# A gated cross-attention stage ahead of six transformer layers: two pairs of groups in a loop become four groups in one written order

## The reference

```python
x = x + tanh(g_xattn[0]) * xattn(layernorm(x), ctx_1024, Wq, bq, qk_b, Wv, bv)
x = x + tanh(g_ffn[0]) * six_layers(layernorm(x), ...)

def xattn(query, value, Wq, bq, qk_b, Wv, bv):
    q = einsum('bsd,ed->bse', query, Wq) + bq + qk_b
    v = einsum('bsd,ed->bse', value, Wv) + bv
    scores = einsum('bqd,bkd->bqk', q, v) / sqrt(128 / 16)
    attn = softmax(scores, axis=-1)
    return einsum('bqk,bkd->bqd', attn, v)
```

## Time and profile before

| what | us or share |
|---|---|
| median of 3 runs (lowest, highest) | 1567.43 (1566.67, 1567.67) |
| the profiled execution's own time | 1565.26 |
| its span, first to last instruction | 1563.4 |
| busy in the span: PE, DVE, ACT, POOL | 96%, 84%, 75%, 76% |
| mean granted clock of PE | 0.983 of 2.4 GHz |

### The profile page before, as it was taken

One profiled execution on the slowest core, in us unless ns is written; L12 is line 12 of the kernel. 1 busy time (PEld: TensorE's weight loads), 2 busy tenths in 40 slices (PEclk: granted clock), 3 DMA queues, 4 the chain that ended last, 5 costly groups with the idle time before them and its releaser, 6 DMA issues.

```text
span 1563.4 us, 80230 instructions
## 1 busy us (share of the span) xinstructions
PE 1499.3 (96%) x31136; PEld 1251.6 (80%) x31136; DVE 1317.1 (84%) x2497; ACT 1167.1 (75%) x2333; POOL 1180.8 (76%) x1166
## 2 busy tenths in 40 slices
PE   4489999999999999999999999999999999999997
PEld 3367888888888888888888888888888888888886
DVE  3578889888888988988888898888889889889883
ACT  3457788788778778877877887887787787777774
POOL 1277877878887887788788878888878877877781
PEclk8789999999999999999999999999999999999998
DMA  5111111011111111101012110112111012010101
GB/s 147 43 43 32 29 37 43 26 50 55 36 30 32 43 40 59 42 27 36 26 43 62 36 42 26 36 32 72 30 32 30 20 31 64 23 30 20 30 25 34
DMA packets 41462, 62.40 MB, mean 40 GB/s; under 512 B 3662, under 2 KB 30412, under 8 KB 41420
## 3 DMA queue, kind: packets, MB, share of 16 engines
q1 hardware_dynamic: 41420, 61.84, 13.5%
HBM read 18.84 MB, written 1.05 MB: 13 GB/s over the span
## 4 chain that ended last, share of the span: by engine, by line
PE 92%; issue 1%; ACT 1%; DVE 0%; POOL 0%; ACTq 0%; DVEq 0%; POOLq 0%
PE bank L1035 16%; PE bank L1105 12%; PE bank L1117 11%; PE bank L1028 10%; PE bank L1029 9%; PE bank L1030 8%; PE bank L1078 8%; PE bank L1152 5%; PE bank L1141 3%; PE bank L1060 3%; PE bank L1142 2%; PE bank L1143 2%; PE bank L1131 1%; PE bank L1125 1%; PE bank L1014 0%
## 5 line engine op out<-in xcount | busy, mean ns | idle before, releaser
L406 POOL TENSOR_TENSOR u<-u,t 128x512 f32<-128x512 f32 x384 | 490.4, 1282 | 23.8 <-DVE t L821 23.8
L420 POOL TENSOR_TENSOR u<-u,rn 128x512 f32<-128x512 f32 x384 | 392.7, 1044 | 75.8 <-ACT rn L572 75.8
L426 POOL TENSOR_TENSOR P<-P,rs 128x512 f32<-128x512 f32 x192 | 196.3, 1043 | 123.6 <-DVE rs L845 123.6
L821 DVE TENSOR_TENSOR t<-bank,TS 128x512 f32<-128x512 f32 x384 | 258.3, 683 | 28.4 <-ACT sq L561 25.8
L1028 PE MATMUL bank<-Wl,xsh 128*128 (+1 forms) x576 | 273.6, 475 | 5.8 <-POOL xsl L400 3.0
L812 DVE TENSOR_TENSOR u<-bank,TC 128x512 f32<-128x512 f32 x384 | 262.1, 683 | 10.1 <-issue 6.5
L805 DVE TENSOR_REDUCE ss<-sq 128x8 f32<-128x512 f32 x384 | 250.5, 673 | 2.9 <-ACT sq L561 2.9
L1029 PE MATMUL bank<-Wh,xsl 128*128 (+1 forms) x576 | 228.4, 397 | 0.0
L1030 PE MATMUL bank<-Wh,xsh 128*128 (+1 forms) x576 | 227.9, 396 | 0.0
L561 ACT ACTIVATE sq<-bank 128x512 f32<-128x512 f32 x384 | 221.5, 605 | 6.2 <-PE bank L1030 5.7
L1035 PE MATMUL bank<-shape_constants,u 128*128 128x128 f32 x1536 | 219.0, 275 | 3.3 <-POOL u L420 3.2
(11 more groups left out here) (102 smaller groups left out, 2960.4 us busy)
## 6 DMA issues: line engine op xcount, KB each, us to landing
vs<-v SPq DMA_DIRECT2D x96, 384.0 KB, 3.3
Wraw<-in_L_ffn_Wqkv_dram SPq DMA_DIRECT2D x72, 117.5 KB, 2.1
WoS<-in_L_ffn_Wo_dram SPq DMA_DIRECT2D x6, 512.0 KB, 3.7
W1h<-Wh SPq DMA_DIRECT2D x6, 341.0 KB, 2.5
W1l<-Wl SPq DMA_DIRECT2D x6, 341.0 KB, 2.9
Wraw<-in_L_ffn_W_dram SPq DMA_DIRECT2D x12, 116.0 KB, 2.2
OT<-in_x_dram SPq DMA_DIRECT2D x2, 512.0 KB, 5.7
v<-in_ctx_dram SPq DMA_DIRECT2D x2, 512.0 KB, 7.0
```

The costliest lines, as they stand in the source:

```text
L406: nc.gpsimd.tensor_tensor(u[:, r, c], u[:, r, c], t2[:, r, c % 2], ALU.add).then_inc(add_done[c], 1)
L420: nc.gpsimd.tensor_tensor(by_head(u[:, r, c]), by_head(u[:, r, c]), spread(rn[:, r, HC * c:HC * c + HC], HC, DH), ALU.mult).then_inc(qk_re ...
L821: nc.vector.tensor_tensor(halves(t2[:, r, c % 2]), halves(bank_of("chunk", c, r)[:])[:, :, ::-1, :], TS[:, layer(it - lag), c % 2].broadca ...
```

## The change

The loop goes. Four groups g = 0 to 3 of four items have temporary tiles and two banks each: `CROSS_A` takes turned x, queries, scores, turned probabilities and the last turn; `CROSS_B` the turned values, the straight values and the attention. Each engine has one written list of steps over all four groups, and every wait counts groups. The arithmetic of a group is the same, instruction by instruction.

- **Inputs in parts.** SP issues eleven transfers ahead of the raw blocks where it were seven: x and context as groups 0, 1, and 2 with 3; the gates, the values' bias and the scales of `ev` apart. PE waits for `fc` and `sc`, DVE for `fc`, ACT for the gates and then `sc`.
- **Context read in place.** PE reads `ctxS`; POOL's copies to `cT` go.
- **POOL** clears `vs[0:32]` (DVE did) and makes the rotary tables at the start, then the eight lower parts, one after another.
- **ACT** takes the upper parts 0 to 3 behind the second group's turned probabilities and 4 to 7 among the last steps, each behind its own block.

The core of the diff (lines that only rename waits and some of the new helpers, which hold the old instructions, are left out):

```diff
-        cT = [t2[:, 0, g] for g in range(2)]
-        slots = [[u[:, g, j] for j in range(NCH)] + [PT[:, 0, g], kT[:, g].rearrange("p t n -> p (t n)")] + [sq[:, g]]
-                 for g in range(2)]
-        xh4, xhT4, qT4, vT4, p4, pT4, v4 = ([slots[g][j] for g in range(2)] for j in range(7))
-        st4 = sb("st4", [128, 2, GB, 6])
-        mv4 = sb("mv4", [128, 2, GB, 2])
-        lv4 = sb("lv4", [128, 2, GB])
-        rstd4 = sb("rstd4", [128, 2, GB])
-        mx4 = sb("mx4", [128, 2, GB])
-        nm4 = sb("nm4", [128, 2, GB])
-        sum4 = sb("sum4", [128, 2, GB])
-        rc4 = sb("rc4", [128, 2, GB])
-        rg4 = sb("rg4", [128, 2, GB])
+        xh4, xhT4 = ([u[:, k, g] for g in range(GROUPS)] for k in range(2))
+        qT4 = [t2[:, g // 2, g % 2] for g in range(GROUPS)]
+        vT4 = [(qT, kT)[g % 2][:, g // 2].rearrange("p t n -> p (t n)") for g in range(GROUPS)]
+        v4 = [PT[:, g // 2, g % 2] for g in range(GROUPS)]
+        p4, pT4 = xh4, xhT4
...
+        CROSS_A, CROSS_B = K[0:4], K[4:8]
...
+        def rows(t, g):
+            return [t[:, GB * g + k] for k in range(GB)]
...
+        def arrived(eng, sems_of_parts, g):
+            eng.wait_ge(sems_of_parts[min(g, 2)], 16)
...
+            def items(t, dst, how, a, b, done):
+                sp.dma_start(dst[:, a:b], t[a:b].rearrange(how)).then_inc(done, 16)
+
+            items(x, H, "b s d -> s b d", 0, GB, x_in[0])
+            sp.dma_start(ev[:, 128:130], every_token[128:130].partition_broadcast(128)).then_inc(gate_in, 16)
+            sp.dma_start(fc[:], by_feature).then_inc(features_in, 16)
+            items(ctxT, ctxS, "b d s -> d b s", 0, GB, ctx_in[0])
+            sp.dma_start(sc[:], shape_consts).then_inc(shapes_in, 16)
+            items(x, H, "b s d -> s b d", GB, 2 * GB, x_in[1])
+            items(ctxT, ctxS, "b d s -> d b s", GB, 2 * GB, ctx_in[1])
+            sp.dma_start(ev[:, 0:128], every_token[0:128].partition_broadcast(128)).then_inc(rows_in, 16)
+            sp.dma_start(ev[:, 130:], every_token[130:].partition_broadcast(128)).then_inc(rows_in, 16)
+            items(x, H, "b s d -> s b d", 2 * GB, NB, x_in[2])
+            items(ctxT, ctxS, "b d s -> d b s", 2 * GB, NB, ctx_in[2])
...
+            nc.gpsimd.memset(vs[0:32], 0.0).then_inc(consts_done, 1)
+            pool.wait_ge(rows_in, 32)
+            pool.wait_ge(shapes_in, 16)
+            pool.sem_inc(wait_met, 1)
...
+            for k in range(NB // 2):
+                lower_part(k, k)
...
+            act.wait_ge(gate_in, 16)
...
+            def cross_rstd(g, s):
+                act.wait_ge(c_mv[s], g + 1)
+                nc.scalar.activation(lv4[:, g], mv4[:, g, :, 1], ACT.Ln, bias=eps_col).then_inc(c_lv[s], 1)
+                act.wait_ge(c_lv[s], g + 1)
+                nc.scalar.activation(rstd4[:, g], lv4[:, g], ACT.Exp, scale=-0.5).then_inc(c_rstd[s], 1)
...
+            def cross_vT_out(g):
+                act.wait_ge(c_vT, g + 1)
+                nc.scalar.activation(vT4[g], CROSS_B[g][:], ACT.Identity, bias=bqc[:, 2:3]).then_inc(c_vTs, 1)
...
+            def cross_q_out(g):
+                act.wait_ge(c_q, g + 1)
+                nc.scalar.activation(qT4[g], CROSS_A[g][:], ACT.Identity, bias=bqs[:]).then_inc(c_qs, 1)
...
+            def cross_exp(g):
+                act.wait_ge(c_nm, g + 1)
+                for t, (dst, src) in enumerate(zip(tiles(p4[g]), tiles(CROSS_A[g]))):
+                    i = nc.scalar.activation(dst, src, ACT.Exp, bias=nm4[:, g, t:t + 1],
+                                             scale=(D / CROSS_HEADS) ** -0.5, accum_out=sum4[:, g, t:t + 1])
+                i.then_inc(c_exp, 1)
...
+            def first_upper(k):
+                act.wait_ge(raw_loaded, 32 * (k + 1))
+                upper_part(k, k)
...
+            act.wait_ge(consts_done, 2)
...
+            cross_rstd(0, 0)
+            cross_vT_out(0)
+            cross_rstd(1, 0)
+            cross_vT_out(1)
+            cross_rstd(2, 0)
+            cross_vT_out(2)
+            cross_x_out(0)
+            cross_rstd(3, 0)
+            cross_vT_out(3)
+            cross_q_out(0)
+            cross_x_out(1)
+            cross_q_out(1)
+            cross_exp(0)
+            cross_x_out(2)
+            cross_x_out(3)
+            cross_p_out(0)
+            cross_exp(1)
+            cross_q_out(2)
+            cross_q_out(3)
+            cross_p_out(1)
+            first_upper(0)
+            first_upper(1)
+            first_upper(2)
+            first_upper(3)
+            cross_exp(2)
+            cross_rstd(0, 1)
+            cross_exp(3)
+            cross_p_out(2)
+            cross_rstd(1, 1)
+            cross_p_out(3)
+            first_upper(4)
+            cross_h_out(0)
+            first_upper(5)
+            cross_h_out(1)
+            first_upper(6)
+            first_upper(7)
+            cross_rstd(2, 1)
+            cross_rstd(3, 1)
+            cross_h_out(2)
+            cross_h_out(3)
...
-            nc.vector.memset(vs[0:32], 0.0)
...
+            dve.wait_ge(features_in, 16)
...
+            def cross_stats(g, s):
+                if s == 0:
+                    arrived(dve, x_in, g)
+                else:
+                    dve.wait_ge(c_x1, g + 1)
+                for t, row in enumerate(rows((H, X1)[s], g)):
+                    i = nc.vector.bn_stats(st4[:, g, t], row)
+                i.then_inc(c_st[s], 1)
+                dve.wait_ge(c_st[s], g + 1)
+                for t in range(GB):
+                    i = nc.vector.bn_aggr(mv4[:, g, t], st4[:, g, t])
+                i.then_inc(c_mv[s], 1)
...
+            def cross_maxima(g):
+                dve.wait_ge(c_sc, g + 1)
+                nc.vector.tensor_reduce(mx4[:, g], by_item(CROSS_A[g][:]), AX, ALU.max).then_inc(c_mx, 1)
+                dve.wait_ge(c_mx, g + 1)
+                nc.vector.tensor_scalar_mul(nm4[:, g], mx4[:, g], -(D / CROSS_HEADS) ** -0.5).then_inc(c_nm, 1)
...
+            cross_stats(0, 0)
+            cross_stats(1, 0)
+            cross_stats(2, 0)
+            cross_norm(0, 0)
+            cross_stats(3, 0)
+            cross_norm(1, 0)
+            cross_norm(2, 0)
+            cross_norm(3, 0)
+            cross_values(0)
+            cross_maxima(0)
+            cross_values(1)
+            cross_values(2)
+            cross_values(3)
+            cross_maxima(1)
+            cross_gates(0)
+            cross_attend(0)
+            cross_gates(1)
+            cross_stats(0, 1)
+            cross_maxima(2)
+            cross_attend(1)
+            cross_maxima(3)
+            cross_stats(1, 1)
+            cross_norm(0, 1)
+            cross_gates(2)
+            cross_gates(3)
+            cross_norm(1, 1)
+            cross_attend(2)
+            cross_attend(3)
+            cross_stats(2, 1)
+            cross_stats(3, 1)
+            cross_norm(2, 1)
+            cross_norm(3, 1)
...
+            def cross_vT(g):
+                arrived(pe, ctx_in, g)
+                nc.tensor.matmul(CROSS_B[g][:], wvT[:], whole(ctxS, g), start=True, stop=True).then_inc(c_vT, 1)
...
+            def cross_v(g):
+                pe.wait_ge(c_vTs, g + 1)
+                for dst, src in zip(tiles(CROSS_B[g]), rows(ctxS, g)):
+                    i = nc.tensor.matmul(dst, src, wvT[:], start=True, stop=True)
+                i.then_inc(c_v, 1)
...
+            def cross_scores(g):
+                pe.wait_ge(c_qs, g + 1)
+                pe.wait_ge(c_vTs, g + 1)
+                for dst, q, w in zip(tiles(CROSS_A[g]), tiles(qT4[g]), tiles(vT4[g])):
+                    i = nc.tensor.matmul(dst, q, w, start=True, stop=True)
+                i.then_inc(c_sc, 1)
...
+            def cross_o(g):
+                pe.wait_ge(c_pTs, g + 1)
+                pe.wait_ge(c_vs, g + 1)
+                for dst, p, w in zip(tiles(CROSS_B[g]), tiles(pT4[g]), tiles(v4[g])):
+                    i = nc.tensor.matmul(dst, p, w, start=True, stop=True)
+                i.then_inc(c_o, 1)
...
+            pe.wait_ge(features_in, 16)
+            pe.wait_ge(shapes_in, 16)
+            cross_vT(0)
+            cross_vT(1)
+            cross_v(0)
+            cross_vT(2)
+            cross_v(1)
+            cross_x(0)
+            cross_vT(3)
+            cross_q(0)
+            cross_x(1)
+            cross_v(2)
+            cross_scores(0)
+            cross_q(1)
+            cross_v(3)
+            cross_x(2)
+            cross_scores(1)
+            cross_x(3)
+            cross_p(0)
+            cross_q(2)
+            cross_o(0)
+            cross_q(3)
+            cross_p(1)
+            cross_scores(2)
+            cross_scores(3)
+            cross_o(1)
+            cross_p(2)
+            cross_p(3)
+            cross_h(0)
+            cross_o(2)
+            cross_o(3)
+            cross_h(1)
+            cross_h(2)
+            cross_h(3)
```

(30 more changed lines are left out.)

219 lines of the change are left out of this document (56 added, 163 removed).

## The result

The changed kernel takes 1542.48 us (median of 4 runs, 1537.95 to 1544.94), the kernel before 1567.05 beside it (4 runs): a ratio of 0.9843, 95% interval [0.9818, 0.9868]. Faster by 1.6%, inside the predicted range, 4.5 us above the predicted 1538.0. The profiled execution took 1542.42 us, 22.8 less than the 1565.26 of before, where 29.1 were predicted. The profile says at once where the difference lies: the start of the layers moved by what was said, and the layers themselves became longer.

The account below looks back on a forecast made before the run. PE bounds the layers, a chain of latencies the cross stage. First layer product from 79.73 to 50.6 us saves 29.1: 1565.26 becomes 1536.2, plus 2.2 for the runs' median, say 1538; range 1532 to 1548.

Parts of the forecast that it names:

- No work goes: Cross stage: PE, ACT and DVE keep their instructions, but for DVE's clearing of a tile; only order and idle time change.
- the copies at nothing: Cross stage: removing POOL's four context copies was priced at nothing, since PE waited for them nowhere.
- Inputs: Start of the kernel: last context part kept at 13.2 us; four more issues could add 3 us, below that 1 us allowed.
- The walk: Cross stage, new lists followed step by step: first layer product at 49.8 or 51.5 us, taken as 50.6 against 79.73 before.
- Exponentials (0): ACT's exponentials of group 0 in the cross stage, forecast from 24.2 to 25.7 us.
- (3): ACT's exponentials of group 3 in the cross stage, forecast behind the maxima from 34.7 to 36.2 us.
- POOL against DVE: Cross stage: POOL's work slows DVE's normalisings beside it; 1 us of that, said to be in the numbers.
- Unrolled code fetches more instructions: Instruction fetch: the unrolled code costs 0 to 1 us more, which no profile row shows.
- The premise that only the start moves: Layers behind the cross stage: they keep their length of 1483.7 us, so all that is saved at the start remains.
- No overlap: Rival, cross stage: passes stay serial, only the 8.86 us wait for weights goes; first product 71 us, total 1558.6; chance 0.035.
- the first rival: Cross stage: PE's clock stays low, every product at low prices; first product 65 us, total 1552.7; chance 0.09.
- The slower rival: Start: the last input part gates every turn of x; slower by over 0.2% if it lands beyond 45.4 us; chance 0.015.

Follow-up runs that it names:

- e1: The changed kernel with 80 small products (160 instructions) more in PE's list, between the turns of groups 1 and 2: 1549.95 us, ratio 0.9899.
- e5: The changed kernel with 48 small products (96 instructions) added while PE waits for its first inputs: 1537.21 us, ratio 0.9822.
- e6: The changed kernel with 104 small products (208 instructions) added while PE waits for its first inputs: 1554.06 us, one run.
- e13: The changed kernel with the first four weight blocks split ahead of ACT's first copy of turned x, as before the change: 1547.20 us, one run.

## Why the prediction was right, and where it was not

**No work goes; the copies at nothing.** This held. With the copies put back the first product came 2.0 us later, but e1, without them and with the same fall of the clock, came 1.75 later; that leaves 0.3 us for the copies (one run each).

**Inputs.** The last context was kept at 13.2 us; PE waited for it until 15.47. Of the 3 us that the prediction's bound allowed for the extra issues, 2.3 were there; SP took 3.54 us for the last issue alone (timeline, columns as in the earlier trace rows):

```profile
6.16 3.54 SPq L321 DMA_DIRECT2D v<-in_ctx_dram  x1
```

**The walk.** That it came out to 0.2 us is luck: the inputs were 2.3 us late, the clock rose early, and e1, with the same lists up to its padding, came 1.75 us later. The prediction had PE low until 19.4 us; the granted clock stands at 1.00 from 15.6 to 36.1. ACT's timeline answers to the earlier trace rows; the rows are the first and last exponentials of group 0, the first of group 3, and the copies to R:

```profile
23.50 0.36 ACT L535 ACTIVATE u<-bank,nm 128x128 f32<-128x128 f32 x1
...
24.77 0.22 ACT L535 ACTIVATION_READ_ACCUMULATOR u<-bank,nm 128x1 f32 x1
...
34.10 0.37 ACT L535 ACTIVATE u<-bank,nm 128x128 f32<-128x128 f32 x1 [0.35 <-DVE nm L816]
...
46.93 2.37 ACT L547 COPY R<-bank 64x512 f32<-64x512 f32 x4 [2.49 <-PE bank L1046]
```

Exponentials (0) were forecast from 24.2 to 25.7 and ran 23.5 to 25.0; (3) from 34.7 and ran from 34.1; the attention of groups 2 and 3 was forecast to end at 39.6 or 41.2 and ended at 37.21 + 3.06 = 40.3, at a mean clock of 0.62; the copies end at 49.3, forecast 48.4 or 50.0; the first product at 50.76, forecast 50.6.

**POOL against DVE.** Forecast 1 us, said to be in the numbers. It is hardly there: from the end of the attention on, the prices as written (normalising at 1.07) give 49.6 or 51.2 us for the first product, where the prediction has 49.8 or 51.5. The last eight normalisings took 2.97 us beside two lower parts (2.42 us from 42.70), and 2.14 with POOL idle; the first four 1.52 beside the tables, for 1.07: 1.3 us in these two (timeline of DVE):

```profile
15.11 1.52 DVE L802 TENSOR_SCALAR u<-OT,mv,rstd 128x128 f32<-128x128 f32 x4
...
43.78 2.97 DVE L802 TENSOR_SCALAR u<-X,mv,rstd 128x128 f32<-128x128 f32 x8
```

**The layers: the step that failed.** "Unrolled code fetches more instructions, a cost that no row shows: 0 to 1 us." The term was sized by how much more code is fetched, and that is one packet (28 for 27). It measured 6 us, because the layers' own straight code moved against the pieces that are fetched, so fetches that had been hidden were no longer, and PE stood for 8.7 us in place of 2.9. The premise that only the start moves is the one that the prediction itself named as what a layer part of another length would break. No kernel here came below the 1483.7 us of before: with the code moved it was 1484.0 us in e5 and 1500.2 in e6 (one run), so the term was 0.3 to 16.5 us, where it was put at 0 to 1. With 6 us there the forecast would have been 1544. The range held the result since it was drawn wide for the walk; for this term that is luck.

**The rivals.** No overlap came to 71 us in the prediction and to 67.3 when forced; the wait for weights, which the prediction took as this rival's only gain, is worth 7.4 to 9.2 us by e13 against the 8.86 of the earlier trace rows. The sign of the first rival showed, products at the low clock past 23 us (from 36.1 to 39.5 and from 42.9 on), but in places where the walk had allowed for it; POOL stayed inside the walk's range. The slower rival needed the last context at 42.3 us or later; its sign, PE idle past 15 us for it, showed for half a microsecond.

## What to carry to other kernels

Work out the start and the steady part of a kernel apart: here a walk through the new lists foresaw the first, helped by errors that cancelled, and nearly all of the error left lay in the part that no edit touched. Before a difference of under one per cent is credited to an edit, shift the program by some tens of harmless instructions and look again: here that moved the time by some 17 us between e5 and e6 (one run), 1.5 of them ahead of the layers. Before a microsecond or two of a start is credited to an edit, look whether the clock was the same: e1 and the changed kernel, alike up to there, differ by 1.75 us. And where a stage is a chain of latencies, look for what the last engines' final steps really need: the first pair's data were ready ten microseconds before they were asked for.

## What the hardware showed that was not expected

PE's program is fetched in packets of 16 KB, one for each 256 instructions: with the loops counted once the changed kernel has some 7,215 records of PE and 28 packets, the kernel before 7,061 and 27. Where a boundary falls into a run of small products (128 in 1.55 us), PE stands for 0.3 to 2.4 us; at 76 of the 81 gaps of the fourteen kernels it goes on 2.2 to 2.9 us behind the packet's start. The Trainium skill (Advanced Engine Details and Errata, "ISA Cache") gives 16 KB and 256 instructions for a line, and 128 KB for TensorE; the trace agrees with the line, and in the loop over the middle steps, some 1,360 instructions of PE each, it shows no such packet between 159 and 1253 us. Not every boundary in dense code stalled, and the places repeated most often at four boundaries' distance; why is open.
